# Moving layer 0's softmax operands into the adjacency stage of a graph-network block, on one Trainium2 core

## The chip, the core and the metric

The kernel runs on one core of a Trainium2 chip. The core has five engines with a queue of instructions each: TensorE (PE: matrix products and transposes into PSUM), VectorE (DVE), ScalarE (ACT), GpSimd (POOL) and SyncE (SP), which here issues the DMA transfers. The engines run side by side and meet only at semaphores. The metric is the device time of one execution in microseconds (us). Before the change it is 1094.26 us, the median of 3 runs (1094.17 to 1097.51).

## The reference

On 625 nodes with 512 features: a layer norm; then three graph convolutions ("layers") over 20625 edges, and beside them a linear-attention mix; then a mixture of 64 experts. The change touches the softmax aggregation of layer 0, cut here to what matters:

```python
def _genconv(x, src, dst, t, w1, b1, lg, lb, w2, b2):
    m = jax.nn.relu(x[src]) + EPS
    z = m * t
    e = jnp.exp(z - zmax[dst])
    denom = jax.ops.segment_sum(e, dst, num_segments=N)
    alpha = e / (denom[dst] + 1e-16)
    agg = jax.ops.segment_sum(alpha * m, dst, num_segments=N)
    h = agg + x
    h = jax.nn.relu(_ln(h @ w1 + b1, lg, lb))
    return h @ w2 + b2
```

The messages depend on the source node alone, so the kernel computes them per node, not per edge. With A the 625 x 625 matrix that counts the edges between two nodes, `denom` is A times e, and the numerator is A times (e * m).

## The kernel before

Nodes are cut into NT = 5 tiles of T = 125. TensorE's products are made from pairs: an operand is split into a rounded part (`_hi`, written by ScalarE as a copy into the rounded type) and its remainder (`_lo`, the original less the rounded part), and `mm3` (lines 254 to 256) sums three products.

The program runs through these stages: layer norm and weights; the attention mix; the **adjacency stage**; layers 0, 1 and 2; shared experts and routing; the 64 routed experts.

The adjacency stage builds A. For each of 5 blocks j of destination nodes it runs 7 passes of G = 5 steps, 35 steps. In a step VectorE writes two one-hot tiles in bf16 (`one_hot_src`, 125 x 626, line 1082, and `one_hot_dst`, 125 x 126, line 1083), and TensorE adds their product in two halves (line 1502). After a block ScalarE takes the counts out of PSUM (`adj_out`, lines 728 and 729), TensorE transposes them (line 1488), ScalarE makes `AT_hi` (lines 737 and 738), and VectorE makes `AT_lo` (`adj_low`, lines 1071 and 1073).

At the head of a layer L stands what I call the **exponential chain**. VectorE lifts the negated maximum (line 1102, semaphore `zmax_neg`). Then for each tile t: ScalarE writes e into `EE` (line 748); VectorE writes the product `EP = EE * HN`, where HN holds the messages (line 1111, semaphore `em`); ScalarE writes `EM[0]` from EP (line 752) and `EX[0]` from EE (line 755); VectorE writes the remainders `EM[1]` (line 1114, semaphore `em_lo`) and `EX[1]` (line 1117, semaphore `e_lo`). TensorE's aggregation (`aggregate`, `mm3` on 125 x 512) waits for `adj_lo`, `e_lo` and `em_lo`.

GpSimd makes layer 0's maximum over all nodes (line 530) once VectorE has the messages of layer 0, which is during the mix (line 923). Its next work is `split_lo_part` (line 370), the remainders of the layer's weights, and `add_x` (line 544). The loads of `w1_00` and `w1_01` are issued by SP after `adj_lo` has counted 5; ScalarE rounds them (`split_hi`, line 352) behind its part of the exponential chain.

The order on each engine is the order in which the code of its block is written out. There is no scheduler.

Of the kernel before, what the change touches and what calls it, by code (L numbers as in the profile page):

```python
# [16 lines left out]
ACT = mybir.ActivationFunctionType  # L17
ALU = mybir.AluOpType
# [4 lines left out]
T = 125  # L23
NT = N // T
# [7 lines left out]
NL = 3  # L32
# [18 lines left out]
LIFT = 40.0  # L51
# [7 lines left out]
def gps_kernel(nc, x, src, dst, cols, rows, w1, w2, cw, wmix, gmix, router, rbias, shared, experts, out):  # L59
# [4 lines left out]
    with ExitStack() as ctx:  # L64
# [12 lines left out]
        def cut(o, n):  # L77
            return slice(o, o + n)
# [3 lines left out]
        def S(name):  # L82
            if name not in sems:
                sems[name] = ctx.enter_context(nc.semaphore(name))
            return sems[name]
# [18 lines left out]
        def pair(o, *dims, p=P):  # L104
            n = 1
            for q in dims:
                n *= q
            return rg(o, *dims, p=p), rg(o + n, *dims, p=p)
# [9 lines left out]
        EX = pair(o_e, NT, D, p=T)  # L118
        EM = pair(o_e + 5120, NT, D, p=T)
        AT_hi = rg(o_at, NT, N, p=T)  # L120
# [38 lines left out]
        HN = fg(0, NT, D, p=T)  # L159
# [6 lines left out]
        EE = [fg(11264 + 512 * i, D, p=T) for i in range(2)]  # L166
        EP = [fg(12288 + 512 * i, D, p=T) for i in range(2)]
# [61 lines left out]
        zmx = sb("zmx", [T, NT + 3], F32)  # L229
# [9 lines left out]
        ps = ctx.enter_context(nc.psum_tensor("ps", [P, 8, 512], F32))  # L239

        pe, dve, act, pool, sp = nc.tensor, nc.vector, nc.scalar, nc.gpsimd, nc.sync

        def f(ap):
            return ap.bitcast(F32)
# [58 lines left out]
        def g1(ins):  # L303

            gstep[0] += 1
            ins.then_inc(S("pool_step"), 1)
            pool.wait_ge(S("pool_step"), gstep[0])
# [181 lines left out]
        def _(eng):  # L489
# [38 lines left out]
            for L in range(NL):  # L528
                pool.wait_ge(S("zmax"), L + 1)
                pool.partition_all_reduce(zmx[:, NT + 1:NT + 2], zmx[:, NT:NT + 1], T, RMAX).then_inc(S("zmax_all"), 1)  # L530
                def mlp_rstd(i):
                    n = NT * L + i
                    rsqrt(mv_m[:, 2:3], mv_m[:, 1:2], 1, "mlp_var", n + 1, "mlp_rstd")
                    pool.wait_ge(S("mlp_rstd"), n + 1)
                    g1(pool.tensor_tensor(mv_m[:, 3:4], mv_m[:, 0:1], mv_m[:, 2:3], ALU.mult))
                    pool.tensor_tensor(mv_m[:, 3:4], zero_c[:], mv_m[:, 3:4], ALU.subtract).then_inc(S("mlp_nmr"), 1)

                def out_rstd(i):
                    if L:
                        rsqrt(mv_o[:, 2:3], mv_o[:, 1:2], 1, "out_var", NT * (L - 1) + i + 1, "out_rstd")  # L540

                def add_x(d):
                    pool.wait_ge(S("quot"), NT * L + d + 1)
                    pool.tensor_tensor(HN[:, d, :], HN[:, d, :], XC[:, d, :], ALU.add).then_inc(S("h"), 1)

                for nme in (f"w1_{L}0", f"w1_{L}1"):
                    for c in range(4):
                        split_lo_part(nme, c, 4)
                add_x(0)
                for c in range(2):  # L550
                    split_lo_part(f"cw_{L}", c, 4)
                add_x(1)
                for c in range(2, 4):
                    split_lo_part(f"cw_{L}", c, 4)
                for d in range(2, 4):
                    add_x(d)
                for c in range(2):
                    split_lo_part(f"w2_{L}0", c, 4)
                add_x(4)
                for c in range(2, 4):  # L560
                    split_lo_part(f"w2_{L}0", c, 4)
                mlp_rstd(0)
                for c in range(4):
                    split_lo_part(f"w2_{L}1", c, 4)
                mlp_rstd(1)
                mlp_rstd(2)
                out_rstd(0)
                mlp_rstd(3)
                out_rstd(1)
                mlp_rstd(4)  # L570
                out_rstd(2)
                out_rstd(3)
                if L == NL - 1:
                    for c in range(4):
                        split_lo_part("sg0", c, 4)
                out_rstd(4)
                if L == NL - 1:
                    for c in range(2):
                        split_lo_part("sd0", c, 2)
# [52 lines left out]
        def _(eng):  # L632
# [90 lines left out]
            def adj_out(j):  # L723

                act.wait_ge(S("adj_ps"), j + 1)
                if j >= 2:
                    act.wait_ge(S("adj_tr"), j - 1)
                act.activation(adj[:, j % 2, 0:313], ps[0:T, 2 * (j % 2), 0:313], ACT.Copy)
                act.activation(adj[:, j % 2, 313:N], ps[0:T, 2 * (j % 2) + 1, 0:312], ACT.Copy).then_inc(S("adj_sb"), 1)


            adj_out(0)
            for j in range(NT):
                if j + 1 < NT:
                    adj_out(j + 1)
                act.wait_ge(S("adj_tr"), j + 1)
                act.activation(AT_hi[:, 0:3, cut(j * T, T)], ps[0:T, 4, 0:3 * T].rearrange("p (s n) -> p s n", s=3), ACT.Copy)
                act.activation(AT_hi[:, 3:5, cut(j * T, T)], ps[0:T, 5, 0:2 * T].rearrange("p (s n) -> p s n", s=2),
                               ACT.Copy).then_inc(S("adj_hi"), 1)

            for L in range(NL):
                act.wait_ge(S("zmax_neg"), L + 1)
                for t in range(NT + 1):
                    n = NT * L + t
                    if t < NT:
                        if t >= 2:
                            act.wait_ge(S("e_lo"), n - 1)
                        act.activation(EE[t % 2], HN[:, t, :], ACT.Exp, scale=colp[0:T, cut(COL_S + 4 + L, 1)],
                                       bias=zmx[:, NT + 2:NT + 3]).then_inc(S("exp"), 1)
                    if t >= 1:  # L750
                        act.wait_ge(S("em"), n)
                        act.activation(EM[0][:, t - 1, :], EP[(t - 1) % 2], ACT.Copy).then_inc(S("em_hi"), 1)
                    if t < NT:
                        act.wait_ge(S("exp"), n + 1)
                        act.activation(EX[0][:, t, :], EE[t % 2], ACT.Copy).then_inc(S("e_hi"), 1)
                for nme in (f"w1_{L}0", f"w1_{L}1"):
                    split_hi(nme)

# [135 lines left out]
        def _(eng):  # L894
# [171 lines left out]


            dve.memset(zero_b, 0.0).then_inc(S("vector_consts"), 1)
            def adj_low(j):
                dve.wait_ge(S("adj_hi"), j + 1)  # L1070
                dve.tensor_tensor(AT_lo[:, 0:3, cut(j * T, T)], ps[0:T, 4, 0:3 * T].rearrange("p (s n) -> p s n", s=3),
                                  f(AT_hi[:, 0:3, cut(j * T, T)]), ALU.subtract)
                dve.tensor_tensor(AT_lo[:, 3:5, cut(j * T, T)], ps[0:T, 5, 0:2 * T].rearrange("p (s n) -> p s n", s=2),
                                  f(AT_hi[:, 3:5, cut(j * T, T)]), ALU.subtract).then_inc(S("adj_lo"), 1)
# [21 lines left out]
            def xi_lo(L, i):  # L1096
                dve.wait_ge(S("xi_hi"), NT * L + i + 1)
                dve.tensor_tensor(XI[i][1], ps[:, 6, 0:4 * T], f(XI[i][0]), ALU.subtract).then_inc(S("xi_lo"), 1)  # L1098

            for L in range(NL):  # L1100
                dve.wait_ge(S("zmax_all"), L + 1)
                dve.tensor_scalar(zmx[:, NT + 2:NT + 3], zmx[:, NT + 1:NT + 2], -1.0, LIFT, ALU.mult, ALU.add).then_inc(S("zmax_neg"), 1)
                if L:
                    xi_lo(L - 1, NT - 1)
                for t in range(NT + 1):
                    n = NT * L + t
                    if t < NT:
                        dve.wait_ge(S("exp"), n + 1)
                        if t >= 2:
                            dve.wait_ge(S("em_lo"), n - 1)  # L1110
                        dve.tensor_tensor(EP[t % 2], EE[t % 2], HN[:, t, :], ALU.mult).then_inc(S("em"), 1)
                    if t >= 1:
                        dve.wait_ge(S("em_hi"), n)
                        dve.tensor_tensor(EM[1][:, t - 1, :], EP[(t - 1) % 2], f(EM[0][:, t - 1, :]), ALU.subtract).then_inc(S("em_lo"), 1)
                    if t < NT:
                        dve.wait_ge(S("e_hi"), n + 1)
                        dve.tensor_tensor(EX[1][:, t, :], EE[t % 2], f(EX[0][:, t, :]), ALU.subtract).then_inc(S("e_lo"), 1)
# [660 lines left out]
```

## Time and profile before

| | |
|---|---|
| median of 3 runs | 1094.26 us |
| profiled execution, its own time | 1095.08 us |
| its span in the trace | 1093.0 us |
| busy: PE, DVE, ACT, POOL | 956.1, 696.7, 449.3, 407.8 us |
| adjacency stage, first one-hot to the last `AT_lo` | 155.68 to 251.87 us |
| first aggregation product of layer 0 | 255.61 us |

The busy time is the sum of the durations of an engine's instructions. The durations of two neighbours on one engine can overlap by about 0.1 us, so the pace of a loop is read from the distance between starts. A bracket at the end of a row of the timeline says how long the engine had been idle before it, and which instruction of which engine ended that. PEclk is the share of TensorE's full clock that was granted: 1.0 is 2.4 GHz and 0.5 is 1.2 GHz.

### The profile page before, as it was taken

How to read it: one execution, taken by the hardware profiler on the slowest of the kernel's cores; microseconds unless marked ns; L12 is line 12 of the kernel's file. 1: busy time of each engine (PE TensorE's matmuls, PEld its weight loads, DVE VectorE, ACT ScalarE, POOL GpSimd, SP SyncE). 2: the span in 40 equal slices, each digit the busy share in tenths (PEclk: the TensorE clock that was granted, in tenths of full speed). 3: DMA queues.
4: the chain of work that ended last, by engine and by line, in shares of the span. 5: the costliest groups of instructions: out<-in, count | busy, mean ns of one | idle time of the engine just before them, and what ended most of it. 6: DMA issues, size and time to landing. Idle time of an engine off the chain costs nothing.

```text
span 1093.0 us, 13131 instructions
## 1 busy us (share of the span) xinstructions
PE 956.1 (87%) x4333; PEld 704.8 (64%) x4333; DVE 696.7 (64%) x1271; ACT 449.3 (41%) x680; POOL 407.8 (37%) x344
## 2 busy tenths in 40 slices
PE   3988789997999999989999679439999999999990
PEld 2888664445888778867887567326666666666650
DVE  4455458995754667786667664317677666766665
ACT  2443400005354525434444211216666666666640
POOL 4500000003530165106513104846566666666540
PEclk9977799998999999999999668859999999999995
DMA  5600013304220132012200440048999999999988
GB/s 164 82 1 1 1 36 121 121 5 145 78 78 0 49 115 78 1 48 87 92 1 0 157 180 2 2 66 300 334 328 333 352 330 342 327 359 340 334 247 219
DMA packets 72945, 160.05 MB, mean 146 GB/s; under 512 B 29686, under 2 KB 37436, under 8 KB 64441
## 3 DMA queue, kind: packets, MB, share of 16 engines
q1 hardware_dynamic: 59641, 147.87, 40.7%
q0 software_dynamic: 13248, 11.45, 3.9%
q8 instruction: 33, 0.54, 0.2%
q14 instruction: 23, 0.19, 0.1%
HBM read 152.83 MB, written 25.76 MB: 163 GB/s over the span
## 4 chain that ended last, share of the span: by engine, by line
PE 65%; DMA 10%; issue 8%; DVE 7%; POOL 5%; ACT 4%; SPq 0%; DVEq 0%; POOLq 0%; ACTq 0%
PE ps L254 15%; PE ps L256 15%; PE ps L255 15%; PE ps L1502 7%; PE ps L1708 7%; DMA expert_weights<-experts_in 7%; POOL slot_scratch L599 3%; PE ps L1690 2%; ACT split_operands L858 1%; DMA split_operands<-yrow_scratch 1%; PE ps L1553 1%; PE ps L1717 1%; DMA x_out<-x_in 1%; PE ps L1416 1%; PE ps L1640 1%
## 5 line engine op out<-in xcount | busy, mean ns | idle before, releaser
L254 PE MATMUL ps<-split_operands 128*125 128x512 f32 (+5 forms) x690 | 275.0, 399 | 35.8 <-DVE split_operands L1098 6.4
L255 PE MATMUL ps<-split_operands 128*125 128x512 f32 (+5 forms) x690 | 267.6, 388 | 0.0
L256 PE MATMUL ps<-split_operands 128*125 128x512 f32 (+5 forms) x690 | 267.3, 387 | 0.0
L620 POOL DMA_INDIRECT yrow_scratch<-work,slots x64 | 142.9, 2234 | 112.9 <-ACT work L874 110.2
L254 PEld LDWEIGHTS ps<-split_operands 128*125 128x125 f32 (+3 forms) x690 | 136.6, 198 | 66.9 <-issue 14.3
L1316 DVE TENSOR_TENSOR gate_up_lo<-expert_weights,split_operands 128x2048 fp32r<-128x2048 f32 x64 | 146.4, 2289 | 31.7 <-ACT split_operands L858 31.5
L370 POOL TENSOR_TENSOR split_operands<-work,split_operands 128x512 fp32r<-128x512 f32 x66 | 85.3, 1321 | 191.6 <-ACT split_operands L352 191.2
L256 PEld LDWEIGHTS ps<-split_operands 128*125 128x125 f32 (+3 forms) x690 | 136.2, 197 | 27.1
L255 PEld LDWEIGHTS ps<-split_operands 128*125 128x125 f32 (+3 forms) x690 | 137.0, 198 | 24.3
L858 ACT ACTIVATE split_operands<-expert_weights 128x2048 fp32r<-128x2048 f32 x64 | 122.2, 1910 | 36.6 <-DMA expert_weights<-experts_in 34.3
L1708 PE MATMUL ps<-expert_weights,work 128*117 128x512 f32 x256 | 120.2, 592 | 0.5 <-issue 0.5
L254 PE MATMUL ps<-split_operands,expert_x 128*117 128x512 f32 x256 | 106.9, 418 | 0.3 <-issue 0.3
L255 PE MATMUL ps<-gate_up_lo,expert_x 128*117 128x512 f32 x256 | 101.6, 397 | 0.0
L256 PE MATMUL ps<-split_operands,expert_x 128*117 128x512 f32 x256 | 101.5, 396 | 0.0
L1502 PE MATMUL ps<-work 125*125 125x313 bf16 x350 | 79.5, 327 | 4.7 <-DVE work L1083 4.1
L614 POOL DMA_INDIRECT work<-xn_scratch,slots x64 | 68.9, 1076 | 25.5 <-issue 25.5
L1126 DVE RECIPROCAL work<-work 125x512 f32<-125x512 f32 x15 | 50.3, 3351 | 38.8 <-ACT work L764 38.8
L1082 DVE TENSOR_SCALAR work<-work 125x626 bf16<-125x626 f16 x175 | 66.8, 382 | 9.1 <-PE ps L1496 8.9
L1708 PEld LDWEIGHTS ps<-expert_weights,work 128*117 128x117 f32 x256 | 46.0, 180 | 39.1 <-issue 32.6
L782 ACT ACTIVATE work<-ps,colp 128x125 f32<-128x125 f32 x120 | 44.0, 468 | 64.3 <-PE ps L1553 64.3
L1502 PEld LDWEIGHTS ps<-work 125*125 125x125 bf16 x350 | 35.5, 138 | 48.8 <-DVE work L1083 48.2
L1329 DVE COPY work<-ps 128x234 f32<-128x234 f32 x64 | 25.7, 402 | 58.4 <-PE ps L1717 58.4
(214 smaller groups left out, 1292.1 us busy)
## 6 DMA issues: line engine op xcount, KB each, us to landing
expert_weights<-experts_in SPq DMA_DIRECT2D x64, 1024.0 KB
expert_weights<-experts_in SPq DMA_DIRECT2D x64, 512.0 KB, 6.7
work<-w_in SPq DMA_DIRECT2D x12, 1024.0 KB, 5.1
yrow_scratch<-work SPq DMA_DIRECT2D x5, 1500.0 KB
split_operands<-yrow_scratch SPq DMA_DIRECT2D x5, 1120.0 KB
work<-wmix_in SPq DMA_DIRECT2D x4, 1024.0 KB, 7.7
work<-cw_in SPq DMA_DIRECT2D x3, 1024.0 KB, 5.2
work<-rows_in SPq DMA_DIRECT2D x10, 256.0 KB, 4.7
```

Of the source, the lines that this page charges most:

```text
L254: pe.matmul(o, a[1], b[0], start=start, stop=False)
L255: pe.matmul(o, a[0], b[1], start=False, stop=False)
L256: return pe.matmul(o, a[0], b[0], start=False, stop=stop)
L370: last = pool.tensor_tensor(v[0], v[1], v[2], ALU.subtract)
L614: pool.indirect_dma_start(XG[e % AHEAD], None, xn2, bass.IndirectOffsetOnAxis(ap=slots[:, e, 0:1], axis=0), bounds_check=last_token, oob_i ...
L620: pool.indirect_dma_start(yrow, bass.IndirectOffsetOnAxis(ap=slots[:, e, 1:2], axis=0), OS[e % 4], None, bounds_check=last_row, oob_is_err ...
L858: act.activation(GU_hi[e % 2], RING[e % RINGS][:, 0:WA], ACT.Copy).then_inc(S("weight_hi"), 1)
L1082: dve.tensor_scalar(one_hot_src[:, i, :], iota_h, srcf[:, bass.ds(lo + q * G + i, 1)], None, ALU.is_equal)
L1126: v1(dve.reciprocal(DEN[d % 2], DEN[d % 2]))
L1316: dve.tensor_tensor(GU_lo[e % RINGS][:], RING[e % RINGS][:, 0:WA], f(GU_hi[e % 2]), ALU.subtract).then_inc(S("weight_lo"), 1)
L1502: last = pe.matmul(ps[0:T, 2 * (j % 2) + h, 0:sn], one_hot_dst[:, i, 0:T], one_hot_src[:, i, cut(s0, sn)], start=False, stop=False)
L1708: last = pe.matmul(ps[0:CAP, 6 + e % 2, :], HTF[e % 2][:, cut(k * CAP, CAP)], RING[e % RINGS][:, cut(WA + 512 * k, 512)], start=(k == 0), ...
```

## The change

For layer 0 alone, the exponential chain now runs before and beside the adjacency stage. VectorE's part of it, the five products and ten remainders, goes to GpSimd. Layers 1 and 2 are as they were.

```diff
@@ gpsimd
                 pool.partition_all_reduce(zmx[:, NT + 1:NT + 2], zmx[:, NT:NT + 1], T, RMAX).then_inc(S("zmax_all"), 1)
+                for t in range(0 if L else NT + 1):
+                    if t < NT:
+                        pool.wait_ge(S("exp"), t + 1)
+                        if t >= 2:
+                            pool.wait_ge(S("em_lo"), t - 1)
+                        pool.tensor_tensor(EP[t % 2], EE[t % 2], HN[:, t, :], ALU.mult).then_inc(S("em"), 1)
+                    if t >= 1:
+                        pool.wait_ge(S("em_hi"), t)
+                        pool.tensor_tensor(EM[1][:, t - 1, :], EP[(t - 1) % 2], f(EM[0][:, t - 1, :]), ALU.subtract).then_inc(S("em_lo"), 1)
+                    if t < NT:
+                        pool.wait_ge(S("e_hi"), t + 1)
+                        pool.tensor_tensor(EX[1][:, t, :], EE[t % 2], f(EX[0][:, t, :]), ALU.subtract).then_inc(S("e_lo"), 1)
@@ scalar: the chain's loop becomes exps(L), called for layer 0 ahead of adj_out(0)
+            exps(0)
             adj_out(0)
...
             for L in range(NL):
+                if L:
+                    exps(L)
                 for nme in (f"w1_{L}0", f"w1_{L}1"):
                     split_hi(nme)
@@ vector
             dve.memset(zero_b, 0.0).then_inc(S("vector_consts"), 1)
+            def lift(L):
+                dve.wait_ge(S("zmax_all"), L + 1)
+                dve.tensor_scalar(zmx[:, NT + 2:NT + 3], zmx[:, NT + 1:NT + 2], -1.0, LIFT, ALU.mult, ALU.add).then_inc(S("zmax_neg"), 1)
+            lift(0)
...
             for L in range(NL):
-                dve.wait_ge(S("zmax_all"), L + 1)
-                dve.tensor_scalar(zmx[:, NT + 2:NT + 3], zmx[:, NT + 1:NT + 2], -1.0, LIFT, ALU.mult, ALU.add).then_inc(S("zmax_neg"), 1)
                 if L:
+                    lift(L)
                     xi_lo(L - 1, NT - 1)
-                for t in range(NT + 1):
+                for t in range(NT + 1 if L else 0):
```

GpSimd's queue between the maximum (line 530 in both) and the first remainders of the weights (line 370), before:

```order
L530 ISA zmx<-zmx 125x1
L370 ISA
L370 TENSOR_TENSOR split_operands<-work,split_operands 128x512 x8
L544 TENSOR_TENSOR work<-work,x_cur 125x512
```

The same place in the changed kernel, where line 536 is the product EP, line 539 the remainder of EM and line 542 the remainder of EX (the first two tiles of five):

```order
L530 ISA zmx<-zmx 125x1
L536 ISA
L536 TENSOR_TENSOR work<-work 125x512
L542 TENSOR_TENSOR split_operands<-work,split_operands 125x512
L536 TENSOR_TENSOR work<-work 125x512
L539 TENSOR_TENSOR split_operands<-work,split_operands 125x512
L542 TENSOR_TENSOR split_operands<-work,split_operands 125x512
```

Fifteen instructions of 125 x 512 now stand ahead of the weights' remainders on GpSimd.

VectorE's queue at the end of the adjacency stage and the start of layer 0, before (the last two `adj_low`, the lift, the chain, the first reciprocal of the quotients):

```order
L1071 TENSOR_TENSOR split_operands<-ps,split_operands 125x3x125
L1073 TENSOR_TENSOR split_operands<-ps,split_operands 125x2x125
L1102 TENSOR_SCALAR zmx<-zmx 125x1
L1111 TENSOR_TENSOR work<-work 125x512
L1117 TENSOR_TENSOR split_operands<-work,split_operands 125x512
L1111 TENSOR_TENSOR work<-work 125x512
L1114 TENSOR_TENSOR split_operands<-work,split_operands 125x512
L1117 TENSOR_TENSOR split_operands<-work,split_operands 125x512
```

and in the changed kernel:

```order
L1096 TENSOR_TENSOR split_operands<-ps,split_operands 125x3x125
L1098 TENSOR_TENSOR split_operands<-ps,split_operands 125x2x125
L1150 RECIPROCAL work<-work 125x512
L1151 TENSOR_TENSOR work<-ps,work 125x512
```

The lift has gone to the front of the adjacency stage, and the chain's fifteen instructions have left VectorE.

ScalarE's queue after the mix (the copies of the attention output, 128x4x125, the last of the mix), in the changed kernel; before, the rows of `adj_out` (125x313 and 125x312) followed the copies directly:

```order
L733 ACTIVATE split_operands<-ps 128x4x125 x5
L752 ACTIVATE work<-work,zmx,colp 125x512
L759 ACTIVATE split_operands<-work 125x512
L752 ACTIVATE work<-work,zmx,colp 125x512
L756 ACTIVATE split_operands<-work 125x512
L759 ACTIVATE split_operands<-work 125x512
```

```order
L756 ACTIVATE split_operands<-work 125x512
L741 ACTIVATE work<-ps 125x313
L742 ACTIVATE work<-ps 125x312
```

The first `adj_out` now stands behind all fifteen of the chain's instructions on ScalarE.

## Rows read from the trace of the kernel before

**Rows 1.** The page: the chain that ended last, by line.
```profile
PE ps L254 15%; PE ps L256 15%; PE ps L255 15%; PE ps L1502 7%; PE ps L1708 7%; DMA expert_weights<-experts_in 7%; POOL slot_scratch L599 3%; PE ps L1690 2%; ACT split_operands L858 1%; DMA split_operands<-yrow_scratch 1%; PE ps L1553 1%; PE ps L1717 1%; DMA x_out<-x_in 1%; PE ps L1416 1%; PE ps L1640 1%
```

**Rows 2.** Groups, 155 to 246 us: busy us, mean ns | idle before, releasers.
```profile
L1082 DVE TENSOR_SCALAR work<-work 125x626 bf16<-125x626 f16 x175 | 66.8, 382 | 9.1 <-PE ps L1496 8.9 <-issue 0.2
L1502 PEld LDWEIGHTS ps<-work 125*125 125x125 bf16 x350 | 35.5, 138 | 48.8 <-DVE work L1083 48.2
```

**Rows 3.** Timeline, 204 to 205 us: start, us, engine, line, operation.
```profile
204.10 0.26 DVE L1083 TENSOR_SCALAR work<-work 125x126 bf16<-125x126 f16 x1
204.27 0.38 DVE L1082 TENSOR_SCALAR work<-work 125x626 bf16<-125x626 f16 x1
204.56 0.26 DVE L1083 TENSOR_SCALAR work<-work 125x126 bf16<-125x126 f16 x1
```

**Rows 4.** Timeline, GpSimd, 262 to 275 us.
```profile
262.85 10.24 POOL L370 TENSOR_TENSOR split_operands<-work,split_operands 128x512 fp32r<-128x512 f32 x8 [152.00 <-ACT split_operands L352]
273.30 1.30 POOL L544 TENSOR_TENSOR work<-work,x_cur 125x512 f32<-125x512 f32 x1 [0.20 <-DVE work L1127]
```

**Rows 5.** Timeline, ScalarE: the chain's first rows, the weights, `adj_out` of blocks 0 and 1.
```profile
172.56 0.43 ACT L728 ACTIVATE work<-ps 125x313 f32<-125x313 f32 x1 [24.45 <-PE ps L1506]
190.84 0.43 ACT L728 ACTIVATE work<-ps 125x313 f32<-125x313 f32 x1 [17.52 <-PE ps L1506]
251.96 0.81 ACT L748 ACTIVATE work<-work,zmx,colp 125x512 f32<-125x512 f32 x1 [1.00 <-DVE zmx L1102]
260.85 3.71 ACT L352 ACTIVATE split_operands<-work 128x2048 fp32r<-128x2048 f32 x2
```

**Rows 6.** Timeline, VectorE and TensorE, 251 to 256 us.
```profile
251.46 0.41 DVE L1073 TENSOR_TENSOR split_operands<-ps,split_operands 125x250 fp32r<-125x250 f32 x1
251.78 0.14 DVE L1102 TENSOR_SCALAR zmx<-zmx 125x1 f32<-125x1 f32 x1
...
254.78 0.68 DVE L1114 TENSOR_TENSOR split_operands<-work,split_operands 125x512 fp32r<-125x512 f32 x1
255.61 0.76 PE L254 MATMUL ps<-split_operands 125*125 125x512 f32 x1 [5.44 <-DVE split_operands L1114]
```

**Rows 7.** Windows: PE, PEld, DVE, ACT, POOL busy, PEclk, DMA share, GB/s.
```profile
248.00:250.20 2.20, 1.38 (x5) 1.12 (x5) 0.64 (x2) 0.00 (x0) 0.00 (x0) 0.60 0.03 7
250.20:255.60 5.40, 0.00 (x0) 0.02 (x1) 3.71 (x8) 4.36 (x8) 0.00 (x0) 0.50 0.48 147
255.60:258.00 2.40, 2.39 (x6) 1.91 (x7) 2.40 (x5) 2.40 (x5) 0.00 (x0) 0.50 1.01 416
...
262.00:293.00 31.00, 31.00 (x139) 24.84 (x138) 17.34 (x11) 8.22 (x10) 20.27 (x16) 1.00 0.33 102
```

**Rows 8.** Timeline, VectorE, 153 to 156 us and first one-hot of block 1.
```profile
153.78 0.27 DVE L1068 MEMSET work<- 125x256 uint32 x1
155.68 0.39 DVE L1082 TENSOR_SCALAR work<-work 125x626 bf16<-125x626 f16 x1 [1.63 <-PE ps L1496]
...
173.96 0.39 DVE L1082 TENSOR_SCALAR work<-work 125x626 bf16<-125x626 f16 x1 [2.24 <-PE ps L1496]
```

**Rows 9.** Timeline, VectorE and GpSimd, 12 to 31 us.
```profile
12.88 0.17 DVE L905 TENSOR_SCALAR mv<-mv 125x5 f32<-125x5 f32 x1
25.76 2.35 DVE L359 TENSOR_TENSOR split_operands<-work,split_operands 128x2048 fp32r<-128x2048 f32 x1 [1.11 <-ACT split_operands L352]
26.04 3.22 POOL L519 TENSOR_TENSOR x_out<-x_out,work 125x512 f32<-125x512 f32 x1
28.03 1.25 DVE L935 TENSOR_SCALAR gb<-colp 128x4 f32<-128x4 f32 x1
29.20 1.33 DVE L936 TENSOR_SCALAR gb<-colp 128x4 f32<-128x4 f32 x1
29.22 1.28 POOL L518 TENSOR_TENSOR x_out<-x_out,work 125x512 f32<-125x512 f32 x1
30.44 1.28 DVE L944 TENSOR_TENSOR work<-ps,work 125x512 f32<-125x512 f32 x2
30.58 1.28 POOL L519 TENSOR_TENSOR x_out<-x_out,work 125x512 f32<-125x512 f32 x1
```

More of the change, by code:

```diff
@@ L729, in adj_out, with exps @@
                 act.activation(adj[:, j % 2, 313:N], ps[0:T, 2 * (j % 2) + 1, 0:312], ACT.Copy).then_inc(S("adj_sb"), 1)
[L732 to L741, printed above, removed]
+            def exps(L):
                 act.wait_ge(S("zmax_neg"), L + 1)
@@ L755, in _ @@
                         act.activation(EX[0][:, t, :], EE[t % 2], ACT.Copy).then_inc(S("e_hi"), 1)
+            exps(0)
+            adj_out(0)
+            for j in range(NT):
+                if j + 1 < NT:
+                    adj_out(j + 1)
+                act.wait_ge(S("adj_tr"), j + 1)
+                act.activation(AT_hi[:, 0:3, cut(j * T, T)], ps[0:T, 4, 0:3 * T].rearrange("p (s n) -> p s n", s=3), ACT.Copy)
+                act.activation(AT_hi[:, 3:5, cut(j * T, T)], ps[0:T, 5, 0:2 * T].rearrange("p (s n) -> p s n", s=2),
+                               ACT.Copy).then_inc(S("adj_hi"), 1)
+            for L in range(NL):
+                if L:
+                    exps(L)
                 for nme in (f"w1_{L}0", f"w1_{L}1"):
```

## The prediction, written before the changed kernel ran

> **What bounds the kernel now.** I read the chain that ended last first. The three lines of `mm3` hold 15% each, the one-hot products of the adjacency stage (line 1502) 7% [rows 1]. A share of the chain does not say who sets TensorE's pace, so the groups of that stage come second. There the weight loads of line 1502 sat idle for 48.8 us, of which VectorE's line 1083 ended 48.2, while VectorE's own idle time in 91 us is 9.1 us, all but 0.2 of it at the starts of blocks [rows 2]. So TensorE waits for VectorE and not the other way round. The timeline gives the pace: line 1083 starts at 204.10 and again at 204.56, so a step takes 0.46 us, and between the two rows line 1082 has no gap around it [rows 3]. VectorE is full, 175 steps long, and whatever holds VectorE in this stage makes the kernel longer by as much. GpSimd has been idle for 152 us when it starts line 370 [rows 4], and ScalarE has been idle for 24.45 us at the first `adj_out` [rows 5]. Those two idle times look like free room.
>
> The third view is the timeline at the seam. The last `AT_lo` ends at 251.87, and the first aggregation product starts at 255.61, released by line 1114 [rows 6]. That distance is what the change can win: the exponentials start only at 251.96 [rows 5], so TensorE waits for the first tile's chain.
>
> **What the change takes away.** With e, EP and their remainders ready, the first aggregation needs `adj_lo` alone. In the row of before TensorE starts 0.15 us behind its releaser (line 1114 ends at 255.46) [rows 6]. So it would start at 251.87 + 0.15 = 252.02 and not at 255.61: 3.6 us earlier. TensorE has no gap in the products that follow (31.00 us busy in the 31 from 262 to 293) [rows 7], and as all five tiles will be ready it has none after the change. Does what hangs on layer 0's start follow by the full 3.6 us? The weights: ScalarE rounds w1 at 260.85, directly behind the chain [rows 5]. With the chain gone it goes on as soon as the loads are in; they fill the DMA engines from about 252 to 260 (busy share 0.48, then 1.01) [rows 7], so ScalarE can begin to round the first half at about 257, takes half of its 3.71 us for it, and GpSimd's 10.24 us begin at about 259.3 and not at 262.85. Before, they end at 273.09 and `add_x` follows at 273.30 once the quotient is there [rows 4]; both move by 3.5 to 3.6. I count 3.6 us.
>
> The clock could add to that. It stands at 0.60 in 248.0 to 250.2 and at 0.50 before and in the first products [rows 7]. It has fallen before the wait in question begins, so a shorter wait need not prevent it: I count nothing. The upper end is that the 2.4 us from 255.6 to 258.0, all at 0.50, run at the full clock in half the time: 1.2 us.
>
> VectorE loses fifteen instructions after 252 us. None of that time is won a second time, since TensorE was already running without gaps behind the first of them. The lift, 0.14 us [rows 6], moves to 154.05, in VectorE's 1.63 us of idle time [rows 8]: free.
>
> **What the change adds to ScalarE.** Fifteen instructions ahead of `adj_out(0)`. They start when the lift is done, about 154.2, and are paced by GpSimd. `adj_out(0)` has its counts at 172.56, but the one who needs it is TensorE between blocks 1 and 2, at about 190, where the next `adj_out` starts at 190.84 [rows 5]. So ScalarE may be late by 18 us before anyone waits. The cover holds if GpSimd gets through twelve of its instructions by then.
>
> **What the change adds to GpSimd.** Fifteen tensor-tensor operations of 125 x 512 with both inputs in SBUF. Lines 518 and 544 are that shape: 1.28 and 1.30 us [rows 4, 9]. Alone they last 15 x 1.28 = 19.2 us, from 155.1 (exponential of 0.81 from 154.2) on. GpSimd has the room. The question is what VectorE does meanwhile, and the trace answers from the one place where both run this kind of work [rows 9]. Line 935 works on four columns. Its like, line 905 with five, takes 0.17 us; line 935 takes 1.25 us and ends at 29.28, with GpSimd's line 519, which ends at 29.26. Line 936 takes 1.33 us and ends at 30.53, with GpSimd's line 518, which ends at 30.50. In the other direction GpSimd's line 519 takes 3.22 us, not 1.28: it was issued at 26.04 inside VectorE's line 359, and what is left after that has ended is one bare duration. The third pair shows an exception: line 944 reads one input from PSUM and runs at its usual 0.64 us a piece beside GpSimd's next instruction. So two instructions that both want SBUF in this way run one after the other, and the small one waits for the whole of the large one.
>
> The Trainium skill states this outright ("SBUF — State Buffer", section on the two separate sides): GpSimd shares a pair of ports with VectorE, as an exclusive lock for a whole instruction, against VectorE instructions that use both of their ports or have two SBUF inputs. Rows 9 agree. The same skill ("VectorE: DVE Perf Modes") counts a 16-bit scalar operation from SBUF to SBUF at four elements a cycle among those that use both ports. By that rule lines 1082 and 1083 are held.
>
> The rows alone: between lines 1083 and 1082 the extra 500 columns cost 0.29 - 0.17 = 0.12 us [rows 3], while line 1114 takes 0.68 for 512 [rows 6]. So line 1082 moves columns several times faster than an ordinary one. It is a tensor-scalar operation from SBUF to SBUF, as 935 and 936 are. I take it to be held as they were.
>
> **The sum.** A hold per GpSimd instruction: lines 935 and 936 together go from 28.03 to 30.44, 2.41 us; less two bare durations of 0.17 that is 2.07, so 1.03 each as the lower end. The upper end is GpSimd's whole 1.28, plus 0.09 for the overlap of neighbours on VectorE that each hold breaks (0.38 long, next start after 0.29 [rows 3]). I take 1.25, nearer to the duration, since here GpSimd's instructions follow each other closely, each as soon as VectorE lets go. The first starts at 155.1 while VectorE waits for TensorE until 155.68 [rows 8], so of its 1.28 only 0.7 counts. Cost: 0.7 + 14 x 1.25 = 18.2 us. VectorE still gets about one instruction in between (0.17 to 0.29 us), so GpSimd's stretch ends near 178, inside block 0, which itself now ends near 190. Hence no block boundary hides any of it, and ScalarE's cover holds.
>
> Net: + 18.2 - 3.6 = + 14.6 us. The profiled execution has 1095.08 us (span 1093.0), which would become 1109.7. It lies 0.8 above the median of the runs; from 1094.26 the forecast is 1108.9, say 1109 us. Its own range: low 0.7 + 14 x 1.03 = 15.1, less 3.6 and 1.2 for the clock, + 10.3, so 1104.6; high 0.7 + 14 x 1.37 = 19.9, + 0.5 for a TensorE that idles to the slower clock and paces a few steps when work returns, less 3.6, + 16.8, so 1111.
>
> **Rivals.**
> A. The one-hot instructions are not held; only operations on 32-bit data are. Place: blocks 0 to 1. For it: no row shows a 16-bit operation beside GpSimd. Against: lines 935 and 936 are the same kind of operation. The cost is 0, the gain stays, 1094.3 - 3.6 = 1090.7, or 1089.5 with the clock. It decides as soon as the hold is under 3.6 / 14.6 = 0.25 us for each GpSimd instruction; below that the kernel is not slower.
> B. VectorE does not let go. Its instructions overlap their neighbours by 0.09 us, with no gap, and GpSimd gets in only where VectorE idles. Then one instruction fits before 155.68 and one in the 2.24 us at 173.96 [rows 8]; after block 1, at 190, TensorE waits for `adj_out(0)`, which stands behind GpSimd's twelfth. Ten instructions, 12.8 us, plus 1.4 for ScalarE, less the 2.2 of idle time there anyway, + 12.0 - 3.6 = + 8.4: 1102.7. Against it: line 518 started at 29.22, just when line 936 (29.20) was issued, and got ahead of it.
> C. A hand-over costs more than seen at 28 us, each about 0.3 us more over fourteen: + 4.2, 1113.
>
> **Numbers.** Forecast 0.68, A 0.13, B 0.12, C 0.07. Within 0.3% (3.3 us, about what a measurement of this kernel can tell from no change) needs a hold between about 0.0 and 0.5 us; A's 3.6 us is just past that bound, so of A's 0.13 I put 0.09 to faster and 0.04 to the same, and 0.02 more from the other cases. Faster 0.09, same 0.06, slower 0.85. The range for 8 in 10 takes in B and C and leaves out A and the tails: 1100 to 1114.
>
> **What would show it.** In the profile after: GpSimd's fifteen between 155 and about 178 at 1.4 to 1.6 us from start to start; in the same stretch VectorE's one-hot rows with durations of 1.2 to 1.6 in place of 0.38 and 0.25, their mean up by 18.2 / 350 = 0.05 us over the stage; `AT_lo` ending at about 270; the first aggregation product 0.15 us behind it; blocks 1 to 4 unchanged at 0.46 us a step. Rival A would show one-hot rows at 0.38 and 0.25 throughout; B, GpSimd's rows stretched far over 1.28 us, its fifteen spread to 190 and beyond, and `adj_out(0)` as the releaser of TensorE. I am wrong on the gain if the first aggregation waits for anything but `adj_lo`, or if layer 0's start is won but w1's remainders then release TensorE.

## The result, and the profile after

The changed kernel takes 1105.48 us, median of 6 runs (1102.15 to 1107.84), against 1094.22 for the kernel before, median of 6 (1093.23 to 1097.51). The ratio is 1.0095, interval 1.0072 to 1.0118: some 10.4 us slower, where 14.6 had been forecast. The profiled execution took 1103.06 us, its span 1101.3.

GpSimd's fifteen instructions, first and last rows (start, duration, engine, line, operation). They answer to the 152 us of idle time in [rows 4]:

```profile
156.58 1.27 POOL L536 TENSOR_TENSOR work<-work 125x512 f32<-125x512 f32 x1 [44.92 <-ACT work L752]
157.82 1.34 POOL L542 TENSOR_TENSOR split_operands<-work,split_operands 125x512 fp32r<-125x512 f32 x1
159.12 1.26 POOL L536 TENSOR_TENSOR work<-work 125x512 f32<-125x512 f32 x1
...
174.28 1.26 POOL L539 TENSOR_TENSOR split_operands<-work,split_operands 125x512 fp32r<-125x512 f32 x1
```

VectorE in the same stretch. These rows answer to [rows 3] and [rows 8]; line 1107 is the one-hot of 626 columns (1082 before), 1108 that of 126 (1083 before):

```profile
157.25 0.79 DVE L1107 TENSOR_SCALAR work<-work 125x626 bf16<-125x626 f16 x1 [1.62 <-PE ps L1520]
157.96 1.26 DVE L1108 TENSOR_SCALAR work<-work 125x126 bf16<-125x126 f16 x1
159.13 1.44 DVE L1107 TENSOR_SCALAR work<-work 125x626 bf16<-125x626 f16 x1
...
174.29 1.43 DVE L1107 TENSOR_SCALAR work<-work 125x626 bf16<-125x626 f16 x1
175.65 0.25 DVE L1108 TENSOR_SCALAR work<-work 125x126 bf16<-125x126 f16 x1
175.81 0.37 DVE L1107 TENSOR_SCALAR work<-work 125x626 bf16<-125x626 f16 x1
```

After the first, each one-hot row beside GpSimd takes about 1.25 us (the narrow one) or 1.43 (the wide one), each starts 0.01 to 0.15 us behind one of GpSimd's, and each ends 0.05 to 0.19 us behind that one's end. With GpSimd's last instruction, which ends at 175.54, they fall back to 0.25 and 0.37. From 157.25 to 175.81 VectorE gets through eight steps. At 0.456 us a step these take 3.7 us; they took 18.6. So 14.9 us are lost here, 0.4 on the first row and 1.04 on each of fourteen. I call what VectorE loses to one instruction of GpSimd a **hold**.

The seam, VectorE and TensorE, which answers to [rows 6] (line 1098 is the last `AT_lo`), and the last two sets of transposes before it, of this kernel:

```profile
266.81 0.41 DVE L1098 TENSOR_TENSOR split_operands<-ps,split_operands 125x250 fp32r<-125x250 f32 x1
```
```profile
262.12 0.78 PE L1512 MATMUL ps<-ident,work 125*125 125x125 f32 x5
264.74 0.78 PE L1512 MATMUL ps<-ident,work 125*125 125x125 f32 x5 [1.84 <-DVE split_operands L1098]
267.27 0.79 PE L254 MATMUL ps<-split_operands 125*125 125x512 f32 x1 [1.75 <-DVE split_operands L1098]
```

and the last set of transposes before the change:

```profile
248.79 1.38 PE L1488 MATMUL ps<-ident,work 125*125 125x125 f32 x5 [1.84 <-DVE split_operands L1073]
```

The first aggregation product now starts 0.05 us behind the last `AT_lo` (3.74 before). From the first one-hot to that product I call the **stage**: 255.61 - 155.68 = 99.9 us before, 267.27 - 157.25 = 110.0 after. The stage explains the result by itself: + 10.1 us, against + 10.4 in the runs. What follows it is unchanged: from the first aggregation product to the start of layer 2's lift (line 1102, 1090 after) it is 231.2 us before and 230.8 after, and 230.8 to 231.4 over the nine profiles other than e5's (232.2 there). From the first aggregation product to the end of the span the profiles differ by up to 6 us (837.4 before, 834.0 after, 832.7 to 838.8 in all), as the runs of one kernel do, so the lengths of whole profiles are not compared here.

The stage starts 1.6 us later in this profile. That is no effect of the change: the `memset` of VectorE ahead of it is later by as much (153.78 before, 155.35 after), and from that to the first one-hot it is 1.90 us in both. Over the eight profiles with nothing put ahead of it, the stage starts between 155.7 and 157.3.

The windows at the end of the stage, after the change (columns as in [rows 7]):

```profile
263.50:265.50 2.00, 0.76 (x5) 0.62 (x5) 0.87 (x2) 0.19 (x1) 0.00 (x0) 1.00 0.00 0
265.50:267.20 1.70, 0.02 (x1) 0.00 (x0) 0.86 (x2) 0.75 (x2) 0.00 (x0) 0.87 0.03 10
267.20:269.20 2.00, 1.93 (x5) 1.54 (x6) 0.01 (x1) 0.00 (x0) 0.00 (x0) 0.50 0.48 35
```

Before, the clock stood at 0.60 in the window of the last transposes [rows 7]; here it is 1.00 in theirs, which took 0.78 and not 1.38 us. The aggregation's first products run at 0.50 in both, for 2.8 us in both.

### The profile page after: what moved, and what is told of

The parts are those of the page before. It is cut to its first block, busy times and chain, and to the rows that moved or that the text cites. A ratio compares the mean times of both kernels' runs of the same rounds, so it can differ in the third digit from the quotient of the medians.

```text
span 1101.3 us, 13131 instructions
## 1 busy us (share of the span) xinstructions
PE 956.8 (87%) x4333; PEld 706.8 (64%) x4333; DVE 702.7 (64%) x1256; ACT 451.1 (41%) x680; POOL 427.8 (39%) x359
## 4 chain that ended last, share of the span: by engine, by line
PE 64%; DMA 10%; DVE 9%; issue 8%; POOL 5%; ACT 4%; DVEq 0%; SPq 0%; POOLq 0%; ACTq 0%
PE ps L254 15%; PE ps L255 14%; PE ps L256 14%; PE ps L1526 7%; PE ps L1732 7%; DMA expert_weights<-experts_in 6%; POOL slot_scratch L612 3%; PE ps L1714 2%; ACT split_operands L876 1%; PE ps L1577 1%; PE ps L1741 1%; DMA split_operands<-yrow_scratch 1%; DVE work L1108 1%; PE ps L1440 1%; DMA yrow_scratch<-work,slots 1%
## 5 line engine op out<-in xcount | busy, mean ns | idle before, releaser
L1526 PE MATMUL ps<-work 125*125 125x313 bf16 x350 | 81.8, 342 | 17.4 <-DVE work L1108 16.8
L1107 DVE TENSOR_SCALAR work<-work 125x626 bf16<-125x626 f16 x175 | 74.0, 423 | 8.6 <-PE ps L1520 8.3
L1526 PEld LDWEIGHTS ps<-work 125*125 125x125 bf16 x350 | 39.0, 146 | 60.2 <-DVE work L1108 58.9
```

The costliest lines, as they stand in the source:

```text
L1107: dve.tensor_scalar(one_hot_src[:, i, :], iota_h, srcf[:, bass.ds(lo + q * G + i, 1)], None, ALU.is_equal)
L1526: last = pe.matmul(ps[0:T, 2 * (j % 2) + h, 0:sn], one_hot_dst[:, i, 0:T], one_hot_src[:, i, cut(s0, sn)], start=False, stop=False)
```

## The experiments

The stage length named with each is read as above, from the one profile of that kernel. Ratios are to the kernel before, and gains named with them are worked out from the ratio. e2, e5, e7 and e8 are one execution each, and their argument rests on their rows.

**e1: all of the chain on VectorE, ahead of the stage.** The GpSimd loop is removed, and VectorE gets:

```diff
             lift(0)
+            for t in range(NT + 1):
+                if t < NT:
+                    dve.wait_ge(S("exp"), t + 1)
+                    if t >= 2:
+                        dve.wait_ge(S("em_lo"), t - 1)
+                    dve.tensor_tensor(EP[t % 2], EE[t % 2], HN[:, t, :], ALU.mult).then_inc(S("em"), 1)
...
```

> GpSimd does none of it: VectorE makes layer 0's fifteen products and remainders itself, all ahead of the first one-hot, right after the lift. Theory (each GpSimd instruction holds VectorE's one-hot instruction for about 1.06 us, 14.9 us in all): VectorE's own fifteen cost 0.60 us each from start to start, 10.3 us from the lift to the last remainder, of which 1.6 us falls into its wait for TensorE. Stage from first one-hot to first aggregation shrinks to about 95 us, the chain in front adds about 8.7, sum + 4 to + 5 against before: about 1099 us, some 6 us faster than the changed kernel, though the engine that is full gets the work. Rival (what costs is that ScalarE's chain stands ahead of the first copy of the counts): no faster than the changed kernel, 1105 us.

Measured: 1101.0 us, ratio 1.0046 (1.0025 to 1.0067), + 5.0 us. VectorE's first and last instruction of the chain and the first one-hot:

```profile
156.21 0.69 DVE L1085 TENSOR_TENSOR work<-work 125x512 f32<-125x512 f32 x1 [0.89 <-ACT work L739]
...
164.81 0.68 DVE L1088 TENSOR_TENSOR split_operands<-work,split_operands 125x512 fp32r<-125x512 f32 x1
166.95 0.39 DVE L1106 TENSOR_SCALAR work<-work 125x626 bf16<-125x626 f16 x1 [1.46 <-issue]
```

The stage shrinks to 262.21 - 166.95 = 95.3 us, and its start moves back by 10.0, not 8.7: from the `memset` ahead of it to the first one-hot it is 11.91 us (155.04 to 166.95) where it was 1.90, since 1.46 us of idle time came again behind the chain. The theory holds, with its size off by 1.3. By the two ratios it is 5.4 us faster than the changed kernel (4.5 by the medians), where some 6 had been expected. The busiest engine does the same fifteen for 0.60 us each, while GpSimd's doing them costs that engine 1.04 each. ScalarE's chain ahead of `adj_out(0)` is in both kernels, so it is not what costs the changed kernel more.

**e2: each GpSimd instruction twice.**

```diff
+                        g1(pool.tensor_tensor(EP[t % 2], EE[t % 2], HN[:, t, :], ALU.mult))
                         pool.tensor_tensor(EP[t % 2], EE[t % 2], HN[:, t, :], ALU.mult).then_inc(S("em"), 1)
...
```

> GpSimd does each of the fifteen instructions twice (same result). Theory: fifteen more holds of about 1.0 to 1.06 us, so from the first one-hot to the first aggregation 110.0 + 15 to 16 = about 125.5 us, and the time about 1119 us. Rival (the one-hot steps lose time to something that does not scale with GpSimd's instructions, as the slower clock of TensorE): stage near 110 us, 1105 us.

Measured: one execution at 1116.66 us, stage 282.20 - 155.83 = 126.4 us. Fifteen more instructions, 16.4 us more stage: the loss goes with their number. The two one-hot rows take 1.43 and 1.29 us until 193.63, where GpSimd ends and line 1110 is back at 0.37:

```profile
191.07 1.43 DVE L1110 TENSOR_SCALAR work<-work 125x626 bf16<-125x626 f16 x1
192.42 1.29 DVE L1111 TENSOR_SCALAR work<-work 125x126 bf16<-125x126 f16 x1
193.63 0.37 DVE L1110 TENSOR_SCALAR work<-work 125x626 bf16<-125x626 f16 x1
```

From 155.83 to 193.63 VectorE gets through fifteen steps, 37.8 us for 6.8 us of work, so it loses 31.0 us to thirty instructions; another 0.6 us of the longer stage is the last set of transposes, which took 1.38 us in this profile and not 0.78.

**e3: the same work in quarters.**

```diff
-                        pool.tensor_tensor(EP[t % 2], EE[t % 2], HN[:, t, :], ALU.mult).then_inc(S("em"), 1)
+                        for c in range(4):
+                            last = pool.tensor_tensor(EP[t % 2][:, cut(128 * c, 128)], EE[t % 2][:, cut(128 * c, 128)], HN[:, t, cut(128 * c, 128)], ALU.mult)
+                        last.then_inc(S("em"), 1)
...
```

> Each of GpSimd's fifteen instructions is cut into four of 128 columns, the same work in sixty. Theory of one in turn (between two GpSimd instructions exactly one VectorE instruction gets through, and its 0.23 us lies inside GpSimd's distance from start to start): a hold is that distance less 0.23 us. At 0.32 to 0.40 us a quarter that is 0.1 to 0.17 us, sixty times, 6 to 10 us in place of 14.9: stage 101 to 105 us, time 1097 to 1101. Rival (VectorE loses GpSimd's whole busy time however it is cut): 15 us or more, stage 110 to 115, time 1105 to 1110.

Measured: 1104.34 us, ratio 1.0087 (1.0058 to 1.0117); stage 265.83 - 156.71 = 109.1 us. GpSimd (four quarters in a row of the view), then VectorE:

```profile
159.60 1.85 POOL L537 TENSOR_TENSOR work<-work 125x128 f32<-125x128 f32 x4
161.41 1.85 POOL L542 TENSOR_TENSOR split_operands<-work,split_operands 125x128 fp32r<-125x128 f32 x4
```
```profile
160.10 0.63 DVE L1113 TENSOR_SCALAR work<-work 125x626 bf16<-125x626 f16 x1
160.65 0.44 DVE L1114 TENSOR_SCALAR work<-work 125x126 bf16<-125x126 f16 x1
161.01 0.62 DVE L1113 TENSOR_SCALAR work<-work 125x626 bf16<-125x626 f16 x1
```

My expectation failed on its number and is right in its form. A quarter takes 0.453 us from start to start (1.81 for four), and a VectorE step, two instructions, 0.905, twice that. So exactly one VectorE instruction gets through per GpSimd instruction. The hold is 0.453 - 0.228 = 0.225 us, where 0.228 is half a step of 0.456; the first quarters ran before the first one-hot, and 58 holds of 0.225 are 13.1 us. I had guessed the quarter at 0.32 to 0.40. The rival's number (a stage of 110 us or more) is nearer to the measured time, and the stage alone would not have told them apart; the rows do.

**e8: the bare quarter.** The kernel before, with `add_x` cut in four in the same way (the diff is that of e3 on line 544), where VectorE runs reciprocals or waits.

> The kernel before with add_x on GpSimd cut into four instructions of 128 columns, where VectorE runs reciprocals or waits: the bare distance from start to start of a quarter. If it is 0.45 us, as it was beside the one-hot instructions in the run with quarters, then VectorE's instruction lay wholly inside it there and the rule of one in turn holds for all sizes; if it is 0.32 to 0.36, GpSimd waited about 0.1 us for VectorE at every turn. Time as before.

```profile
274.58 1.72 POOL L545 TENSOR_TENSOR work<-work,x_cur 125x128 f32<-125x128 f32 x4 [0.45 <-DVE work L1129]
276.25 2.53 POOL L370 TENSOR_TENSOR split_operands<-work,split_operands 128x512 fp32r<-128x512 f32 x2
```

From the start of the four quarters to that of the next row it is 1.67 us, 0.42 each. Beside the one-hot instructions it was 0.453. So GpSimd lost only 0.035 us at each turn, and VectorE's 0.16 to 0.29 us lay almost wholly inside GpSimd's own distance. One execution, 1097.0 us.

**e4: VectorE makes them in its own idle time.** Nothing on GpSimd; tile j's three instructions stand behind block j, ScalarE's part is spread to match.

```diff
                 if j >= 2:
                     adj_low(j - 2)
+                chain_product(j)
+                if j >= 1:
+                    chain_em_lo(j - 1)
             adj_low(NT - 2)
+            chain_em_lo(NT - 1)
             adj_low(NT - 1)
```

> GpSimd does none of it. ScalarE's part is spread over the adjacency stage, and VectorE's fifteen stand between the blocks, tile j after block j, where it waits 1.6 to 2.2 us for TensorE; the last tile's lie among the last two AT_lo. Theory: each group of three lasts 1.8 us and fits the wait at least in large part, so 0 to 3 us are added to the stage; the first aggregation follows the last AT_lo by 0.05 us as in the changed kernel, 3.7 us won. Stage 96 to 99 us in place of 99.9; time 1090.5 to 1093.5. Rival (the wait at a block's start is VectorE's own register loads and would only move back): the fifteen add their whole 9 us, stage about 105, time 1099.

Measured: 1091.56 us, ratio 0.9966 (0.9950 to 0.9983): 3.7 us faster than before, 14 faster than the changed kernel by the two ratios. Stage 252.50 - 156.97 = 95.5 us. The group of line 1126 (626 columns) shows where the room came from: its idle time at the blocks' starts is 2.8 us, where it was 9.1 before [rows 2]. Of both, 1.6 us lie ahead of the first one-hot, so 6.3 us were filled within the stage. The rest of the fifteen's 9.0 went into VectorE's waits for ScalarE before the last two sets of `AT_lo`, 1.15 us here and 4.1 before.

```profile
L1126 DVE TENSOR_SCALAR work<-work 125x626 bf16<-125x626 f16 x175 | 67.0, 383 | 2.8 <-PE ps L1543 2.8
```

The end of the stage, with the last tile's instructions (lines 1112, 1114, 1118) between the pieces of `AT_lo` (1103, 1105):

```profile
247.11 0.69 DVE L1112 TENSOR_TENSOR work<-work 125x512 f32<-125x512 f32 x1
247.71 0.69 DVE L1114 TENSOR_TENSOR split_operands<-work,split_operands 125x512 fp32r<-125x512 f32 x1
248.31 0.69 DVE L1118 TENSOR_TENSOR split_operands<-work,split_operands 125x512 fp32r<-125x512 f32 x1
248.95 0.55 DVE L1103 TENSOR_TENSOR split_operands<-ps,split_operands 125x375 fp32r<-125x375 f32 x1
...
251.57 0.55 DVE L1103 TENSOR_TENSOR split_operands<-ps,split_operands 125x375 fp32r<-125x375 f32 x1 [1.15 <-ACT split_operands L771]
```

The rival of that expectation, that the wait only moves back, is refuted here, though in e1 a wait of 1.46 us did come again behind a chain put all in front.

**e5: the one-hot instructions read PSUM.** As the changed kernel, with the numbers to compare copied to two free banks:

```diff
+            iota_p = ps[0:T, 6:8, :].rearrange("p b n -> p (b n)")
+            v1(dve.tensor_copy(iota_p[:, 0:N + 1], iota_h))
...
-                        dve.tensor_scalar(one_hot_src[:, i, :], iota_h, srcf
+                        dve.tensor_scalar(one_hot_src[:, i, :], iota_p[:, 0:N + 1], srcf
```

> As the changed kernel, but the numbers that the one-hot instructions compare come from PSUM in fp32, so that these instructions read no tensor from SBUF. Each is slower by itself (about 0.75 us for 626 columns). Theory (the two engines exclude each other over the way into SBUF): the rows beside GpSimd's fifteen are as long as the rows later in the stage, and GpSimd's fifteen keep 1.26 us; the stage is long, about 175 x 0.85 to 0.95 = 150 to 170 us, and free of holds. Rival (a running GpSimd instruction stops VectorE whatever it reads): rows beside GpSimd of 1.2 us or more against about 0.75 later.

Measured: one execution at 1193.08 us, stage 358.61 - 158.13 = 200.5 us; longer than I had said, since a step takes 1.03 us, and I had left out the 20 us of the stage that lie outside its steps. What it was run for is in the rows beside GpSimd (VectorE's, then GpSimd's):

```profile
160.20 0.86 DVE L1109 TENSOR_SCALAR work<-ps,work 125x626 bf16<-125x626 f32 x1
160.98 0.34 DVE L1110 TENSOR_SCALAR work<-ps,work 125x126 bf16<-125x126 f32 x1
161.24 0.86 DVE L1109 TENSOR_SCALAR work<-ps,work 125x626 bf16<-125x626 f32 x1
```
```profile
159.60 1.26 POOL L539 TENSOR_TENSOR split_operands<-work,split_operands 125x512 fp32r<-125x512 f32 x1
160.82 1.26 POOL L542 TENSOR_TENSOR split_operands<-work,split_operands 125x512 fp32r<-125x512 f32 x1
```

and a step later in the stage, with GpSimd idle:

```profile
190.15 0.88 DVE L1109 TENSOR_SCALAR work<-ps,work 125x626 bf16<-125x626 f32 x1
190.93 0.36 DVE L1110 TENSOR_SCALAR work<-ps,work 125x126 bf16<-125x126 f32 x1
```

Steps of 1.04 us beside GpSimd and 1.03 without it, so no trace of a hold, and GpSimd at 1.22 from start to start, against 1.26 in the changed kernel. GpSimd does not stop VectorE as such. It stops instructions that take their tensor from SBUF as the one-hot ones do. This experiment changed two things at once, the place (PSUM for SBUF) and the type of the input (32 bits for 16). That the type alone does not free VectorE is shown by lines 935 and 936, 32-bit scalar operations from SBUF, which were held all the same (1.25 and 1.33 us for four columns) [rows 9].

**e6: the first tile alone.** GpSimd gets three of the fifteen, the rest stays on VectorE behind the stage.

```diff
+                if L == 0:
+                    pool.wait_ge(S("exp"), 1)
+                    pool.tensor_tensor(EP[0], EE[0], HN[:, 0, :], ALU.mult).then_inc(S("em"), 1)
...
```

> Of layer 0's chain only the first tile's three instructions go to GpSimd ahead of the adjacency stage, the other tiles stay on VectorE behind it. Theory: two holds of 1.03 us and 0.5 us of the first, 2.6 us lost; the first aggregation follows the last AT_lo directly, 3.7 us won, and the second tile is ready before TensorE is through with the first at its slow clock. Stage about 95.3 + 2.6 = 98 us against 99.9 before; time 1092.5 to 1094. Rival (the whole win needs all tiles): TensorE waits for the second tile by some 2 us, no gain, 1095 us or more.

Measured: 1092.24 us, ratio 0.9984 (0.9971 to 0.9998), stage 253.99 - 155.79 = 98.2 us. As expected: TensorE needs only the first tile to start. Its products follow one another without a gap from 253.99 on, and the whole gain is had for three holds (2.5 us) and not fifteen. That makes it a little faster than before, by 1.7 us. The interval ends just short of 1.

**e7: GpSimd only writes.** The fifteen are memsets of the same tiles; layer 0's products and remainders are zero.

```diff
-                        pool.tensor_tensor(EP[t % 2], EE[t % 2], HN[:, t, :], ALU.mult).then_inc(S("em"), 1)
+                        pool.memset(EP[t % 2], 0.0).then_inc(S("em"), 1)
...
```

> The fifteen GpSimd instructions are replaced by memsets of the same tiles: GpSimd writes 125 x 512 and reads nothing (the products and remainders of layer 0 are zero, so that part of the computation is left out). Theory: a write holds VectorE's one-hot instructions too, at 0.5 us each from start to start less 0.23, about 4 us in all: stage 99 us. Rival (only a GpSimd instruction that reads SBUF holds it): the one-hot rows stay at 0.38 and 0.25, stage 95.5 us.

Measured: one execution at 1094.23 us, stage 255.31 - 156.23 = 99.1 us, 3.8 above e1's 95.3. VectorE, then GpSimd:

```profile
159.05 0.60 DVE L1107 TENSOR_SCALAR work<-work 125x626 bf16<-125x626 f16 x1
159.57 0.60 DVE L1108 TENSOR_SCALAR work<-work 125x126 bf16<-125x126 f16 x1
159.72 0.60 DVE L1107 TENSOR_SCALAR work<-work 125x626 bf16<-125x626 f16 x1
```
```profile
156.18 0.53 POOL L542 MEMSET split_operands<- 125x512 f32 x1
...
159.38 0.73 POOL L539 MEMSET split_operands<- 125x512 f32 x1
160.06 0.73 POOL L542 MEMSET split_operands<- 125x512 f32 x1
```

Writing holds VectorE too, and the stage came out at the theory's 99 us, in part by luck. The turn is another one than it took: a step (two VectorE instructions) takes 0.675 us, just the distance of one memset. So two instructions get through per memset, and the hold is 0.675 - 0.456 = 0.22 us, not 0.27. By the rows VectorE loses 3.2 us in all (156.23 to 165.65); 0.6 more are longer idle times at the blocks' starts than in e1. The memset is slowed too: 0.73 us, where one that started before the first one-hot took 0.53.

## Why the prediction was right, and where it was off

*What bounds.* Right: VectorE paces the adjacency stage. 14.9 us of holds on VectorE at its beginning are all in the stage's length: it is 110.0 us against e1's 95.3 without them (e2: twice the holds, 31 us above 95.3, of which 0.6 are its slower transposes).

*The hold itself.* Right, and shown. It rested on two rows of four columns at 28 us [rows 9]. The description of the chip ahead of the prediction says that the engines meet only at semaphores; these rows show VectorE and GpSimd meeting at SBUF as well. Rival A (16-bit one-hot rows not held) is refuted by the rows after; e5 takes the hold away by moving the tensor input to PSUM, and e2 scales it.

*Its size: the term that was mis-sized.* I put 0.7 + 14 x 1.25 = 18.2 us, it was 0.4 + 14 x 1.04 = 14.9. The measured hold is the lower end of my own bounds, 1.03. I chose 1.25, "nearer to the duration", on the ground that the two engines follow each other closely. But lines 935 and 936 had already shown turns of both engines, and gave 1.03 (2.41 us for two turns, less VectorE's own time). I took VectorE's instruction and GpSimd's as times that add up; e3 and e8 show that the VectorE instruction of each turn lies within GpSimd's distance from start to start (0.453 against 0.42 bare for a quarter, 1.26 against 1.22 for the whole in e5). What VectorE loses per turn is GpSimd's distance less its own. That is 3.3 of the 4.2 us by which I forecast too much. The Trainium skill ("SBUF — State Buffer", the two separate sides) has the loser blocked fully, for the other's whole instruction. For VectorE the rows agree: it gets done only 0.05 to 0.19 us behind the end of GpSimd's instruction. For GpSimd they show next to nothing of such a block, 0.04 us a turn beside a VectorE instruction of 0.16 to 0.29.

*GpSimd's stretch* should have lasted from 155.1 to near 178 at 1.4 to 1.6 us a turn; it lasted from 156.58 to 175.54 at 1.26, 19.0 us and not 22.9, for the same reason.

*The gain.* 3.6 us forecast, 3.7 measured at the seam (0.05 us behind the releaser, not 0.15). e1, e4, e6 and the changed kernel all show it, and layer 0 passes it on: ScalarE rounds the first half of w1 as its load lands, 5.0 us behind the last `AT_lo`, and GpSimd starts line 370 at 274.22, 7.0 us behind it (11.0 before, from [rows 4] and [rows 6]).

*The clock.* I counted nothing, and for the aggregation's first products that was right. The last set of transposes took 0.6 us less than before, but that is not shown to be an effect of the change. The set took 0.78 us in the profiles of the changed kernel, e1, e4 and e7, 1.04 in e6, 1.28 in e3 and in e8, whose stage is as before, and 1.38 before, in e2 and in e5. So it goes neither with where the chain runs nor with the length of the stage, and there is one profile of each. What sets it is open. Another 0.5 us of the stage went with shorter idle times at the blocks' starts (VectorE 8.6 in all, 9.1 before); why they are shorter is open too. The sum for this pair of profiles: + 14.9 - 3.7 - 0.6 - 0.5 = + 10.1. The mis-sized hold (3.3), these two (1.1) and the seam (0.1) make 4.5 us between + 14.6 and + 10.1; the runs, at + 10.4, make it 4.2.

*Free parts.* The lift, and ScalarE's chain ahead of `adj_out(0)`: ScalarE was done at 172.5, and the first `adj_out` ran at 189.04 as soon as TensorE had the counts. Right.

*Rivals B and C.* VectorE let go at every instruction, so B did not happen. A turn lost 1.04 us, as at 28 us (1.03), and not 0.3 more than I had counted (C).

## What to carry to other kernels

An idle GpSimd is not free room while VectorE is the engine that paces and its instructions are scalar operations from SBUF to SBUF like the one-hot ones here: each tensor-tensor instruction of GpSimd costs VectorE that instruction's distance from start to start less one instruction of its own. Work out both prices before moving work off VectorE; here 0.60 us on VectorE became 1.04 us on VectorE plus GpSimd's own time. Look first for gaps in the pacing engine's own timeline (9.1 us at the blocks' starts here, 7.5 of them within the stage), and ask how much of the moved work is needed to release the waiting engine: three of the fifteen were.

## What was not expected of the hardware

- In turns with a tensor-tensor instruction of GpSimd, VectorE's instruction costs GpSimd only about 0.04 us (1.26 against 1.22 for 512 columns, 0.453 against 0.42 for 128), while the turn costs VectorE nearly all of GpSimd's instruction (1.04 of 1.26 us).
- Cutting the GpSimd instructions in four hardly helped (a stage of 109.1 us for 110.0): bare, a quarter takes 0.42 us from start to start (e8) and a whole one 1.22 (e5). By my estimate from these two that is 0.15 us fixed and 2.1 ns a column.
- A memset on GpSimd, which reads no tensor, holds VectorE's 16-bit instructions as well, but lets two of them through per memset (0.22 us lost per memset), and is itself slowed from 0.53 to 0.73 us (e7).
